# A mixture-of-experts kernel: small tiles moved as 128 rows, and the rotation tables made later on VectorE

## The chip, the cores and the metric

One core of one Trainium2 chip runs the whole program. The metric is the device time of one execution in microseconds (us), the median of the runs.

## The reference

Three blocks in a row on x of 4096 rows (tokens) by 256 columns: the same feed-forward layer twice, with a state-space layer between them.

```python
x = x + 0.5 * ffn(layernorm(x));  x = x + ssm(layernorm(x));  x = x + 0.5 * ffn(layernorm(x))
# ffn: each token goes to the one expert of E = 8 with the largest logit
router_probs = softmax(x @ Wr);  expert_idx = argmax(router_probs);  p_max = max(router_probs)
h = gelu(x @ W1[e] + b1[e]);  out = p_max * (h @ W2[e] + b2[e])      # D = 256, F = 1024
# ssm: N = 128 diagonal complex states, over the 4096 rows in order
h = a_disc * h + B_disc @ u_t;  y_t = Re(C @ h_t)
```

## The kernel before

The weights of all experts are loaded and split into two float16 parts at the start. A routing stage sorts the tokens by expert and makes a list of NT = 39 tiles of up to 128 tokens for each feed-forward layer. Tiles 0 to 31 have 128 slots. Tiles 32 to 38 have `width(q)` = 16 * (39 - q) slots: 112, 96, 80, 64, 48, 32 and 16. A slot with no token has the index 4095 for gathers and an index beyond the table for scatters, which the bounds check drops. A layer of the kernel is called the first (before the state-space layer) or the second.

Each layer's `ffn` is one loop over the tiles, written out on four engines that meet at semaphores:

- GpSimd (POOL) gathers the tile's rows of x (`xg`) and its records (`recf`) six tiles ahead, and scatters its result (`og`, two buffers). `fetch(q)` is two indirect DMAs at line 384, `scatter(q)` one at line 391. Its queue runs scatter(q), fetch(q + 6), scatter(q + 1), and so on.
- ScalarE (ACT) normalises (L521), writes the high half of the turned tile (L537), and applies the gelu, eight instructions per tile (L552).
- TensorE (PE) runs, in turn q: the transposes of tile q + 2 (L1135), `product1(q + 1)` (48 matmuls, L1160, as many columns as the tile is wide), and `product2(q)` (24 matmuls of 256 columns, L1180 to L1182). `product1(q + 1)` waits for VectorE's split of that tile; `product2(q)` for VectorE's split of the gelu output.
- VectorE (DVE) runs, in turn q: `split_x(q + 2)` (a register load of the expert's number, then L873), `split_h(q + 1)` (L885, L888, twice), `result(q)` (L902, L905, and in the first layer the statistics L908 and L909, after which it raises `o`, on which the scatter waits).

In the first layer VectorE also makes the tables `turn` and `back` of the state-space layer behind `result(q)`: `double(n)` (L705 to L708) doubles the table's length from n to 2n in four instructions; after nine of them it has 512 columns. Turns q = 8 to 16 hold double(1) to double(256); turn 18 clears `state` (L925); turns 20 and 22 hold the two `readout` calls (L714 and L715 over 512 columns each). Their first reader is VectorE itself in the state-space layer (L1016, L1028).

Behind the first layer SyncE (SP) waits for all scatters, then reads the rows back (L327). VectorE's next work, `negative_means` (L1008), waits for those loads.

Of the kernel before, what the change touches and what calls it, by code (L numbers as in the profile page):

```python
# [20 lines left out]
U32 = mybir.dt.uint32  # L21
# [7 lines left out]
T = 4096  # L29
D = 256  # L30
# [9 lines left out]
NT = NJ + E - 1  # L40
# [3 lines left out]
RW = D + 2  # L44
NB = E + 1
GR = 8
RING = 6
# [14 lines left out]
class Chain:  # L62
# [5 lines left out]
    def link(self, instruction):  # L68

        instruction.then_inc(self.sem, 1)  # L70
        self.n += 1
        self.engine.wait_ge(self.sem, self.n)


def macaron(nc, A):
# [3 lines left out]
    rec_dram = {ph: nc.dram_tensor(f"records_{ph}", [T, 4], F32, kind="Internal").ap() for ph in (1, 2)}  # L79
    x2_dram = nc.dram_tensor("x_after_ssm", [T, D], F32, kind="Internal").ap()  # L80
    ctx = ExitStack()
    with ctx:
        def sb(name, shape, dt=F32):
            return ctx.enter_context(nc.sbuf_tensor(name, shape, dt))
# [31 lines left out]
        state = sb("state", [P, 2])  # L116
# [16 lines left out]
        sorti = sb("sorti", [P, NT, 3], I32)  # L133
        eid = sb("eid", [P, NT], I32)

        def view(at, *shape, dt=F32):

            size = 1
            for s in shape:
                size *= s  # L140
            words = size // 2 if dt in (F16, BF16) else size
            assert at + words <= ARENA
            a = big[:, 2 * E * WB + 4 * at:2 * E * WB + 4 * (at + words)].bitcast(dt)
            names = "abcd"[:len(shape)]
            if len(shape) == 1:
                return a
            return a.rearrange("p (" + " ".join(names) + ") -> p " + " ".join(names),
                               **{n: s for n, s in zip(names, shape)})
# [26 lines left out]
        og = [view(6144 + k * RW, RW) for k in range(2)]  # L175
        xg = [view(8192 + k * D, D) for k in range(RING)]
# [15 lines left out]
        recf = sb("recf", [P, RING, 4])  # L192
# [60 lines left out]
        def width(q):  # L253

            return P if q < NJ else STEP * (NT - q)
# [83 lines left out]
        def _(pool):  # L339
# [27 lines left out]
            def ffn(ph, src, dst):  # L367
                s = S[ph]
                table = src
                pool.wait_ge(s["sorted_sb"], 1)  # L370
                if ph == 2:
                    for k in range(2):
                        pool.wait_ge(s_stored[k], 16 * (NC // 2))

                def fetch(q):

                    k, w = q % RING, width(q)
                    if q >= RING:
                        pool.wait_ge(s["o"], q - RING + 1)
                    for to, source, index in ((xg[k][0:w], table, 0), (recf[0:w, k, :], rec_dram[ph], 1)):  # L380
                        if index == 1 and q == 0:
                            pool.wait_ge(s["sorted_all"], 1)
                            pool.wait_ge(s["rec_stored"], 16)
                        pool.indirect_dma_start(to, None, source, bass.IndirectOffsetOnAxis(  # L384
                            ap=sorti[0:w, q, index:index + 1].bitcast(U32), axis=0)).then_inc(s["gath"][k], 16)

                def scatter(q):

                    w = width(q)
                    pool.wait_ge(s["o"], q + 1)  # L390
                    pool.indirect_dma_start(dst, bass.IndirectOffsetOnAxis(ap=sorti[0:w, q, 2:3].bitcast(U32), axis=0),  # L391
                                            og[q % 2][0:w, 0:RW if ph == 1 else D], None, bounds_check=T - 1, oob_is_err=False) \
                        .then_inc(s["scat"][q % RING], 16)

                for q in range(RING):
                    fetch(q)
                for q in range(NT):
                    scatter(q)
                    if q + RING < NT:
                        fetch(q + RING)  # L400
# [213 lines left out]
        def _(dve):  # L614
            chain = Chain(dve, dve_chain)
            link = chain.link
# [84 lines left out]
            def double(n):  # L701

                c0, s0 = turn[:, 0, 0:n], turn[:, 1, 0:n]
                cn, sn = turn[:, 0, n - 1:n], turn[:, 1, n - 1:n]
                dve.tensor_scalar(back[:, 0, 0:n], s0, sn, None, ALU.mult)  # L705
                link(dve.tensor_scalar(back[:, 1, 0:n], c0, sn, None, ALU.mult))
                dve.scalar_tensor_tensor(turn[:, 0, n:2 * n], c0, cn, back[:, 0, 0:n], ALU.mult, ALU.subtract)
                link(dve.scalar_tensor_tensor(turn[:, 1, n:2 * n], s0, cn, back[:, 1, 0:n], ALU.mult, ALU.add))  # L708

            def readout(part):  # L710

                col_a, col_b, how = (0, 1, ALU.subtract) if part == 0 else (1, 0, ALU.add)
                tmp = aa[:, part, :]
                link(dve.tensor_scalar(tmp, turn[:, col_b, :], col(15), None, ALU.mult))  # L714
                link(dve.scalar_tensor_tensor(back[:, part, :], turn[:, col_a, :], col(14), tmp, ALU.mult, how))  # L715
# [145 lines left out]
            def ffn(ph):  # L861
                s = S[ph]
                dve.wait_ge(owners, ph)
                experts = {}

                def split_x(q):

                    e = experts[q] = dve.value_load(eid[0:1, q:q + 1], min_val=0, max_val=E - 1)
                    w = width(q)
                    src = bank[6 + q % 2][:, 0:DC * P].rearrange("p (c t) -> p c t", c=DC)[:, :, 0:w]  # L870
                    sc = xscale[:, bass.ds(e, 1)]
                    dve.wait_ge(s["xt_hi"], q + 1)
                    dve.scalar_tensor_tensor(xts[q % 2][:, 1, :, 0:w], src, sc, xts[q % 2][:, 0, :, 0:w], ALU.mult, ALU.subtract) \  # L873
                        .then_inc(s["xt"], 1)

                def split_h(q):

                    sc = hscale[:, bass.ds(experts[q], 1)]
                    if q >= 2:
                        dve.wait_ge(s["m2"], q - 1)  # L880
                    for half in range(2):
                        f = slice(4 * half, 4 * half + 4)
                        dve.wait_ge(s["gelu"], q * 2 + half + 1)
                        of = slice(0, width(q))
                        dve.tensor_scalar(hs[q % 2][:, 0, f, of], hb[q % 2][:, f, of], sc, None, ALU.mult) \  # L885
                            .then_inc(s["h_hi"], 1)
                        dve.wait_ge(s["h_hi"], q * 2 + half + 1)
                        dve.scalar_tensor_tensor(hs[q % 2][:, 1, f, of], hb[q % 2][:, f, of], sc,  # L888
                                                 hs[q % 2][:, 0, f, of], ALU.mult, ALU.subtract).then_inc(s["hsplit"], 1)

                def result(q):

                    e = experts[q]
                    if q == 0:
                        dve.wait_ge(s["b2in"], 16)
                    dve.wait_ge(s["m2"], q + 1)
                    if q >= 2:
                        dve.wait_ge(s["scat"][(q - 2) % RING], (q - 2) // RING * 16 + 16)
                    w = width(q)
                    o, acc = og[q % 2][0:w, 0:D], bank[4 + q % 2][0:w, 0:D]  # L900
                    i2 = inv2[0:w, bass.ds(e, 1)]
                    dve.scalar_tensor_tensor(o, acc, i2, b2b[0:w, bass.ds(e * D, D)], ALU.mult, ALU.add) \  # L902
                        .then_inc(s["o_chain"], 1)
                    dve.wait_ge(s["o_chain"], q + 1)
                    last = dve.scalar_tensor_tensor(o, o, recf[0:w, q % RING, 2:3], xg[q % RING][0:w], ALU.mult, ALU.add)  # L905
                    if ph == 1:
                        link(last)
                        link(dve.bn_stats(stats[0:w, q % 2, :], o))  # L908
                        last = dve.bn_aggr(og[q % 2][0:w, D:D + 2], stats[0:w, q % 2, :])  # L909
                    last.then_inc(s["o"], 1)  # L910

                split_x(0)
                split_x(1)
                split_h(0)
                for q in range(NT):
                    if q + 2 < NT:
                        split_x(q + 2)
                    if q + 1 < NT:
                        split_h(q + 1)
                    result(q)  # L920
                    if ph == 1:
                        if 8 <= q < 17:
                            double(1 << (q - 8))
                        if q == 18:
                            link(dve.memset(state[:], 0.0))  # L925
                        if q in (20, 22):
                            readout((q - 20) // 2)

            entry_stats(3)
            weight_scales(0)  # L930
# [363 lines left out]
```

## Time and profile before

| | |
|---|---|
| median of 3 runs | 633.14 us (630.43 to 636.55) |
| profiled execution, own time | 628.32 us |
| its span | 626.4 us, mean granted TensorE clock 0.915 |
| TensorE, VectorE, ScalarE, GpSimd busy | 88%, 74%, 66%, 46% of the span |
| chain that ended last, by engine | TensorE 73%, VectorE 14% |

The span runs from the first to the last instruction; the execution's own time is 1.92 us more. A change of under 1% (6.3 us) can't be told from none by the measured times alone.

### The profile page before, as it was taken

Reading aid. Unit: us, or ns where it says so; the run is one execution under the profiler, and the core shown is the slowest. Engines: PE = TensorE matmul, PEld = TensorE weight load, DVE = VectorE, ACT = ScalarE, POOL = GpSimd, SP = SyncE. Lnnn points to the kernel's source line nnn. Section 1 sums busy time; section 2 is a strip of 40 time slices with the busy share of each in tenths; the row PEclk is TensorE's granted clock in tenths of the full one; section 3 lists DMA queues with packets and bytes.
Section 4 is the critical chain, followed back from the end, with each engine's and each line's share of the span. In section 5 each row is a group of like instructions: output and inputs, shape, how many; then the busy total and the mean of one; then the engine's idle time right before and its main releaser. Section 6 shows DMA issues by size and latency. Waiting matters only on the chain.

```text
span 626.4 us, 18541 instructions
## 1 busy us (share of the span) xinstructions
PE 548.9 (88%) x6476; PEld 500.8 (80%) x6476; DVE 465.1 (74%) x1001; ACT 412.1 (66%) x966; POOL 285.3 (46%) x326
## 2 busy tenths in 40 slices
PE   5990119999998999999989998799999999999991
PEld 5990019999998999999747776699999999999990
DVE  6759996888888888887529998576766666776760
ACT  3896997667675676677355663386667776667760
POOL 0042055555545455554245143555555555555521
PEclk9555558999999999999998989799999999999996
DMA  7999021111111111110081213111111111111100
GB/s 262 369 376 353 7 84 35 53 53 54 44 44 52 40 48 51 50 40 20 3 270 37 98 68 135 33 51 45 53 53 52 48 47 44 53 50 44 28 8 0
DMA packets 34616, 50.99 MB, mean 81 GB/s; under 512 B 6603, under 2 KB 27862, under 8 KB 34272
## 3 DMA queue, kind: packets, MB, share of 16 engines
q1 hardware_dynamic: 24800, 31.93, 14.9%
q0 software_dynamic: 9728, 17.89, 9.8%
q8 instruction: 55, 0.90, 0.6%
q14 instruction: 33, 0.27, 0.1%
HBM read 37.05 MB, written 13.67 MB: 81 GB/s over the span
## 4 chain that ended last, share of the span: by engine, by line
PE 73%; DVE 14%; issue 4%; DMA 3%; ACT 3%; SPq 1%; POOL 1%; POOLq 0%; DVEq 0%; ACTq 0%
PE banks L1160 31%; PE banks L1180 11%; PE banks L1182 11%; PE banks L1181 11%; PE banks L1093 3%; PE banks L1135 3%; DVE weights_arena L1019 3%; DMA weights_arena<-L_attn_u 2%; DVE weights_arena L662 2%; PE banks L1065 1%; DVE weights_arena L1016 1%; DVE weights_arena L1000 1%; ACT weights_arena L477 1%; DVE weights_arena L1028 1%; ACT weights_arena L468 1%
## 5 line engine op out<-in xcount | busy, mean ns | idle before, releaser
L552 ACT ACTIVATE weights_arena<-banks,b1t,inv 128x128 f32<-128x128 f32 (+7 forms) x624 | 220.7, 459 | 33.3 <-PE banks L1160 32.9
L1160 PE MATMUL banks<-weights_arena 128*128 128x128 f16 (+7 forms) x3744 | 206.9, 214 | 3.1 <-DVE weights_arena L873 2.0
L1160 PEld LDWEIGHTS banks<-weights_arena 128*128 x3744 | 199.3, 98 | 6.9 <-issue 5.9
L1180 PE MATMUL banks<-weights_arena 128*128 (+7 forms) x624 | 170.2, 273 | 0.0
L1182 PE MATMUL banks<-weights_arena 128*128 (+7 forms) x624 | 170.1, 273 | 0.0
L1181 PE MATMUL banks<-weights_arena 128*128 (+7 forms) x624 | 170.1, 273 | 0.0
L885 DVE TENSOR_SCALAR weights_arena<-weights_arena,hscale 128x512 f16<-128x512 f32 (+4 forms) x156 | 75.4, 483 | 54.5 <-ACT weights_arena L552 53.4
L888 DVE SCALAR_TENSOR_TENSOR weights_arena<-weights_arena,hscale 128x512 f16<-128x512 f32 (+4 forms) x156 | 109.9, 704 | 5.5
L537 ACT ACTIVATE weights_arena<-banks,xscale 128x256 f16<-128x256 f32 (+7 forms) x78 | 35.6, 456 | 92.3 <-PE banks L1135 89.9
L384 POOL DMA_INDIRECT recf<-records,sorti x78 | 83.3, 1067 | 23.8 <-issue 23.8
L391 POOL DMA_INDIRECT x_after_ffn<-weights_arena,sorti x39 | 39.4, 1010 | 82.9 <-DVE weights_arena L909 82.9
L391 POOL DMA_INDIRECT out<-weights_arena,sorti x39 | 39.1, 1003 | 75.3 <-DVE weights_arena L905 69.7
L1182 PEld LDWEIGHTS banks<-weights_arena 128*128 128x128 f16 (+7 forms) x624 | 62.4, 100 | 6.4
L1180 PEld LDWEIGHTS banks<-weights_arena 128*128 128x128 f16 (+7 forms) x624 | 62.4, 100 | 5.8
L1181 PEld LDWEIGHTS banks<-weights_arena 128*128 128x128 f16 (+7 forms) x624 | 62.4, 100 | 5.6
L873 DVE SCALAR_TENSOR_TENSOR weights_arena<-banks,xscale,weights_arena 128x256 f16<-128x256 f32 (+7 forms) x78 | 35.9, 460 | 41.3 <-issue 23.6
L384 POOL DMA_INDIRECT weights_arena<-L_attn_u,sorti x39 | 41.4, 1062 | 31.8 <-DVE sorti L854 20.2
L521 ACT ACTIVATE weights_arena<-weights_arena,recf 128x256 f32<-128x256 f32 (+7 forms) x78 | 46.1, 591 | 6.6 <-DMA recf<-records,sorti 6.6
L384 POOL DMA_INDIRECT weights_arena<-x_after_ssm,sorti x39 | 38.7, 992 | 17.0 <-issue 11.6
L902 DVE SCALAR_TENSOR_TENSOR weights_arena<-banks,inv,weights_arena 128x256 f32<-128x256 f32 (+7 forms) x78 | 37.3, 478 | 5.0 <-PE banks L1182 4.9
L662 DVE SCALAR_TENSOR_TENSOR weights_arena<-weights_arena,wscale 128x2048 f16<-128x2048 f32 x16 | 37.3, 2339 | 3.8 <-ACT weights_arena L477 3.7
L905 DVE SCALAR_TENSOR_TENSOR weights_arena<-weights_arena,recf 128x256 f32<-128x256 f32 (+7 forms) x78 | 37.8, 484 | 2.8
(216 smaller groups left out, 626.3 us busy)
## 6 DMA issues: line engine op xcount, KB each, us to landing
weights_arena<-L_ffn_W SPq DMA_DIRECT2D x16, 1024.0 KB, 12.7
weights_arena<-x_after_ffn SPq DMA_DIRECT2D x8, 516.0 KB, 7.4
weights_arena<-L_attn_u SPq DMA_DIRECT2D x8, 512.0 KB, 10.5
x_after_ssm<-weights_arena SPq DMA_DIRECT2D x8, 512.0 KB, 2.9
weights_arena<-L_ffn_b SPq DMA_DIRECT2D x2, 1024.0 KB, 5.2
recf<-records,sorti POOLq DMA_INDIRECT x78, 2.6
weights_arena<-L_attn_u,sorti POOLq DMA_INDIRECT x39, 3.0
x_after_ffn<-weights_arena,sorti POOLq DMA_INDIRECT x39, 2.5
```

Source lines behind the costliest of these rows:

```text
L384: pool.indirect_dma_start(to, None, source, bass.IndirectOffsetOnAxis(ap=sorti[0:w, q, index:index + 1].bitcast(U32), axis=0)).then_inc(s[ ...
L391: pool.indirect_dma_start(dst, bass.IndirectOffsetOnAxis(ap=sorti[0:w, q, 2:3].bitcast(U32), axis=0), og[q % 2][0:w, 0:RW if ph == 1 else ...
L521: act.activation(xng[q % 2][0:w], xg[q % RING][0:w], ACT.Identity, bias=recf[0:w, q % RING, 0:1], scale=recf[0:w, q % RING, 1:2]).then_inc ...
L552: last = act.activation(hb[q % 2][:, f, 0:width(q)], src, ACT.Gelu, bias=b1t[:, bass.ds(e * FC + f, 1)], scale=inv1[:, bass.ds(e, 1)])
L662: dve.scalar_tensor_tensor(lo, raw(e, which), wscale[:, n:n + 1], hi, ALU.mult, ALU.subtract) \
L885: dve.tensor_scalar(hs[q % 2][:, 0, f, of], hb[q % 2][:, f, of], sc, None, ALU.mult) \
L888: dve.scalar_tensor_tensor(hs[q % 2][:, 1, f, of], hb[q % 2][:, f, of], sc, hs[q % 2][:, 0, f, of], ALU.mult, ALU.subtract).then_inc(s["hs ...
L905: last = dve.scalar_tensor_tensor(o, o, recf[0:w, q % RING, 2:3], xg[q % RING][0:w], ALU.mult, ALU.add)
L1160: last = pe.matmul(acc[:, f * P:f * P + n_cols], weights[wpart * DC + d], xts[q % 2][:, xpart, d, 0:n_cols], start=(n == 0), stop=(n == 5))
L1180: pe.matmul(acc, hs[q % 2][:, 0, f, of], high, start=(f == 0), stop=False)
L1181: pe.matmul(acc, hs[q % 2][:, 0, f, of], low, start=False, stop=False)
L1182: last = pe.matmul(acc, hs[q % 2][:, 1, f, of], high, start=False, stop=(f == FC - 1))
```

## The change

Two edits. Every gather and scatter moves 128 rows, also for the seven narrow tiles, where it moved `width(q)`. The computation keeps its widths. And the doublings of the tables go from turns 8 to 16 to turns 28 to 36 (NT - 11 to NT - 3), the clearing of `state` and both readouts from turns 18, 20 and 22 to behind the last tile of the first layer; the clearing has no wait of its own any more.

```diff
 def fetch(q):
-    k, w = q % RING, width(q)
+    k = q % RING
...
-    for to, source, index in ((xg[k][0:w], table, 0), (recf[0:w, k, :], rec_dram[ph], 1)):
+    for to, source, index in ((xg[k], table, 0), (recf[:, k, :], rec_dram[ph], 1)):
...
-            ap=sorti[0:w, q, index:index + 1].bitcast(U32), axis=0)).then_inc(s["gath"][k], 16)
+            ap=sorti[:, q, index:index + 1].bitcast(U32), axis=0)).then_inc(s["gath"][k], 16)
 def scatter(q):
-    w = width(q)
...
-    pool.indirect_dma_start(dst, bass.IndirectOffsetOnAxis(ap=sorti[0:w, q, 2:3].bitcast(U32), axis=0),
-                            og[q % 2][0:w, 0:RW if ph == 1 else D], None, bounds_check=T - 1, oob_is_err=False) \
+    pool.indirect_dma_start(dst, bass.IndirectOffsetOnAxis(ap=sorti[:, q, 2:3].bitcast(U32), axis=0),
+                            og[q % 2] if ph == 1 else og[q % 2][:, 0:D], None, bounds_check=T - 1, oob_is_err=False) \
...
         if ph == 1:
-            if 8 <= q < 17:
-                double(1 << (q - 8))
-            if q == 18:
-                link(dve.memset(state[:], 0.0))
-            if q in (20, 22):
-                readout((q - 20) // 2)
+            if NT - 11 <= q < NT - 2:
+                double(1 << (q - NT + 11))
+    if ph == 1:
+        dve.memset(state[:], 0.0)
+        readout(0)
+        readout(1)
```

## Rows read from the trace of the kernel before

**Rows 1.** The page: busy time, share of the span, instructions.

```profile
PE 548.9 (88%) x6476; PEld 500.8 (80%) x6476; DVE 465.1 (74%) x1001; ACT 412.1 (66%) x966; POOL 285.3 (46%) x326
```

**Rows 2.** The chain that ended last, in order of time: start us, us, what.

```profile
100.21 2.69 PE banks L1160 x48
...
202.31 2.85 PE banks L1160 x48
...
285.01 1.83 PE banks L1160 x48
...
289.71 1.51 PE banks L1160 x48
...
294.08 1.30 PE banks L1160 x48
...
298.35 1.30 PE banks L1160 x48
...
302.38 1.29 PE banks L1160 x48
...
407.60 2.85 PE banks L1160 x48
...
606.19 1.31 PE banks L1160 x48
```

**Rows 3.** Timeline of VectorE: first instruction of a tile's turn; start us, us.

```profile
153.06 0.48 DVE L873 SCALAR_TENSOR_TENSOR weights_arena<-banks,xscale,weights_arena 128x256 f16<-128x256 f32 x1 [0.77 <-DVE turn L708]
...
158.92 0.48 DVE L873 SCALAR_TENSOR_TENSOR weights_arena<-banks,xscale,weights_arena 128x256 f16<-128x256 f32 x1 [0.79 <-DVE turn L708]
...
176.54 0.48 DVE L873 SCALAR_TENSOR_TENSOR weights_arena<-banks,xscale,weights_arena 128x256 f16<-128x256 f32 x1 [0.78 <-DVE turn L708]
...
182.50 0.48 DVE L873 SCALAR_TENSOR_TENSOR weights_arena<-banks,xscale,weights_arena 128x256 f16<-128x256 f32 x1 [0.78 <-DVE turn L708]
...
188.53 0.48 DVE L873 SCALAR_TENSOR_TENSOR weights_arena<-banks,xscale,weights_arena 128x256 f16<-128x256 f32 x1 [0.77 <-DVE turn L708]
...
194.76 0.48 DVE L873 SCALAR_TENSOR_TENSOR weights_arena<-banks,xscale,weights_arena 128x256 f16<-128x256 f32 x1 [0.78 <-DVE turn L708]
...
201.40 0.48 DVE L873 SCALAR_TENSOR_TENSOR weights_arena<-banks,xscale,weights_arena 128x256 f16<-128x256 f32 x1 [0.77 <-DVE turn L708]
...
212.36 0.48 DVE L873 SCALAR_TENSOR_TENSOR weights_arena<-banks,xscale,weights_arena 128x256 f16<-128x256 f32 x1 [0.78 <-DVE state L925]
...
217.37 0.48 DVE L873 SCALAR_TENSOR_TENSOR weights_arena<-banks,xscale,weights_arena 128x256 f16<-128x256 f32 x1 [0.56 <-issue]
...
261.08 0.48 DVE L873 SCALAR_TENSOR_TENSOR weights_arena<-banks,xscale,weights_arena 128x256 f16<-128x256 f32 x1 [0.56 <-issue]
```

**Rows 4.** Groups of VectorE by shape, 92 to 320 us: busy us, mean ns | idle.

```profile
L888 DVE SCALAR_TENSOR_TENSOR weights_arena<-weights_arena,hscale 128x512 f16<-128x512 f32 x64 | 48.1, 752 | 2.3
...
L885 DVE TENSOR_SCALAR weights_arena<-weights_arena,hscale 128x512 f16<-128x512 f32 x64 | 32.7, 512 | 5.0 <-ACT weights_arena L552 4.7
...
L888 DVE SCALAR_TENSOR_TENSOR weights_arena<-weights_arena,hscale 128x64 f16<-128x64 f32 x2 | 0.6, 284 | 0.1
...
L885 DVE TENSOR_SCALAR weights_arena<-weights_arena,hscale 128x64 f16<-128x64 f32 x2 | 0.5, 255 | 0.6 <-ACT weights_arena L552 0.6
```

**Rows 5.** Timeline of VectorE at the end of the first layer.

```profile
309.19 0.47 DVE L902 SCALAR_TENSOR_TENSOR weights_arena<-banks,inv,weights_arena 16x256 f32<-16x256 f32 x1 [0.98 <-PE banks L1182]
...
317.36 0.17 DVE L1008 TENSOR_SCALAR nb<-weights_arena 128x4 f32<-128x4 f32 x1 [6.54 <-DMA weights_arena<-x_after_ffn]
```

**Rows 6.** Timeline of GpSimd: the scatter beside the first readout.

```profile
222.63 1.23 POOL L391 DMA_INDIRECT x_after_ffn<-weights_arena,sorti  x1 [1.47 <-DVE weights_arena L909]
```

**Rows 7.** Line 391, first layer: ns min/median/max; landing us over both layers.

```profile
L391 POOL DMA_INDIRECT x_after_ffn<-weights_arena,sorti x39: 850/1012/1230, 109.2 to 311.6; - x39
...
DMA to landing us min/median/max: 1.8/2.5/4.0
```

**Rows 8.** DMA queues, 300 to 316 us: packets, MB, share.

```profile
q0 software_dynamic: 128, 0.00, 0.4%
```

## The prediction

> **What bounds the kernel now.** I read the page first, then the chain that ended last, then VectorE's timeline. TensorE is busy for 88% of the span [rows 1], and the chain runs through its matmuls nearly all the way through both feed-forward layers. The reader should look at the starts of `product1`: in the second layer they come every 5.52 us for full tiles, which is TensorE's own pace. From product1(1) to product1(38) the second layer takes 606.19 - 407.60 = 198.59 us, the first 302.38 - 100.21 = 202.17 us [rows 2]. The matmuls are the same, so the first layer loses 3.6 us somewhere.
>
> VectorE's timeline says where. Its turn without extra work is 217.37 - 212.36 = 5.01 us when it waits for nobody, 0.5 us under TensorE's 5.52. A turn with a doubling is longer than TensorE's: 158.92 - 153.06 = 5.86 us with double(2), (176.54 - 158.92) / 3 = 5.87 with each of double(4), (8) and (16), then 5.96, 6.03, 6.23 and 6.64 with double(32), (64), (128) and (256) [rows 3]. The extra over 5.01 is thus 0.86 us for the small ones, most of it fixed cost of four instructions and two waits, and 0.95, 1.02, 1.22, 1.63 for the last four. TensorE feels this once VectorE's lead is used up: product1(19) starts at 202.31, 0.91 us after the turn's first instruction at 201.40 [rows 2, 3], and it was waiting for just that instruction. So one number does the work below: product1(q + 2) can't start before the start of VectorE's turn q plus 0.91 us (0.48 is the instruction, 0.43 the way to TensorE).
>
> **What goes.** Turns 8 to 22 lose all extra work. Their turns fall to 5.01 us against 5.52, TensorE keeps its pace, and the first layer regains its 3.6 us. What is late next there is TensorE itself, so no more than this can be won.
>
> **What comes in turns 28 to 36.** The same nine doublings cost VectorE the same there, but the tiles get narrower from q = 32, and so does TensorE's turn. The starts of product1(34) to (38) are 285.01, 289.71, 294.08, 298.35, 302.38, so the turns are 4.70, 4.37, 4.27 and 4.03 us [rows 2]. VectorE's turn shrinks too. The split instructions fall from 752 to 284 ns and from 512 to 255 ns over seven steps of 16 tokens [rows 4], 0.067 and 0.037 each; twice a turn that is 0.20 us per step for `split_h(q + 1)`. `split_x(q + 2)` handles two columns per token where each split handles four, so half a step of 0.067, 0.03 us (an estimate from the same price per column). Its turns 30 to 35 without extra are then 4.98, 4.74, 4.51, 4.27, 4.04 and 3.81 us.
>
> Now add up from turn 28, which starts at 261.08 on the clock of before [rows 3] (TensorE's starts are kept on that clock too, the 3.6 us being taken off at the end):
> - turn 29 at 266.94 (+5.86), 30 at 272.81 (+5.87), 31 at 278.65 (+4.98 + 0.86), 32 at 284.25 (+4.74 + 0.86), 33 at 289.62 (+4.51 + 0.86), 34 at 294.84 (+4.27 + 0.95), 35 at 299.90 (+4.04 + 1.02), 36 at 304.93 (+3.81 + 1.22).
> - With the 0.91 us less 0.03 for each narrower step of its instruction, product1 may start, for tile 34, at 285.06 (before: 285.01), for 35 at 290.40 (+0.69), 36 at 295.58 (+1.50), 37 at 300.61 (+2.26), 38 at 305.61 (+3.23).
>
> VectorE's lead over TensorE thus covers double(1) to double(8) and is used up at turn 32 (285.06 against 285.01), before the long ones come, at the turns in which TensorE is fastest. Behind them, double(256) stands between `result(36)` and `split_h(38)`. Turn 36 without the next register load (0.56 us [rows 3]) is 3.57 - 0.56 = 3.0 us, with the doubling 4.63, so `split_h(38)` starts at 309.56, its first half is done at 310.1, and with 0.43 us for the way product2(38) starts at 310.5. Before, it started a turn behind product1(38), 302.38 + 4.03 = 306.4, and the last result's first instruction at 309.19 [rows 5], 2.8 us later. So the last result starts at 313.3 instead of 309.19: 4.1 us lost.
>
> **Both together:** -3.6 + 4.1 = +0.5 us. The cost moves, and is about as large at its new place, since the slack per turn is no larger (5.52 - 5.01 = 0.51 us for full tiles; 4.03 - 3.6 = 0.4 us for the narrowest).
>
> **The readouts behind the last tile.** Each is two instructions over 512 columns, by the same shapes some 0.75 + 0.51 us [rows 4], both 2.5 to 2.8 us with their waits. VectorE stands idle for 6.54 us there until the first rows are read back at 317.36 [rows 5]; they fit in. Without that cover they would cost the 2.8 us. The cleared `state` is small and has no wait of its own: nothing.
>
> But the last scatter is issued in this same stretch, and the way from it through the read-back is the path. Beside the first readout of before a scatter took 1.23 us [rows 6], against a median of 1.012 and a least of 0.850 (the last one, of 16 rows) [rows 7]. The Trainium skill, SBUF — State Buffer, section "SBUF: two separate sides", says that VectorE and GpSimd hold one port pair exclusively for a whole instruction, and that descriptors of GpSimd's DMAs can't be written meanwhile; the row with 1.23 us agrees in kind.
>
> **128 rows for narrow tiles.** GpSimd's instruction goes from 0.85 us (16 rows) towards 1.01 us (128 rows), 0.16 us at most per DMA [rows 7]. It is hidden for 20 of the 21 DMAs a layer (three for each of seven tiles): the gathers run six tiles ahead, the scatters have two turns until their buffer is wanted. GpSimd is busy for 46% [rows 1]. On the path it counts at the last scatter of each layer. The landing could at most go from 1.8 to the median of 2.5 us [rows 7]. The last four scatters moved 0.00 MB [rows 8]: with all their indices dropped, they have nothing to write, and the added slots are also dropped, so I take the landing unchanged (0) and keep 0.7 us per layer for the range. First layer: 1.23 - 0.85 = 0.38 us with the readout beside it; second: 0.16 us.
>
> **Sum** against the profiled execution of 628.32 us (span 626.4, the 1.92 us outside unchanged): -3.6 + 4.1 + 0.38 + 0.16 = +1.0, so 629.4 us. That execution was 0.8% faster than the median of the three runs; in the median's terms 633.1 + 1.0 = 634.1 us.
>
> **Rivals.**
> - *The early gain stays.* If doublings in the narrow turns cost less than in full ones, or VectorE's lead at turn 28 is larger, only a small part of the 4.1 us comes back: with 1 us lost, 634.1 - 3.1 = 631.0. For it: VectorE waited 0.98 us for TensorE before the last result [rows 5], so there is slack at the end. Against: that slack is counted above, and the fixed cost of a doubling has no reason to shrink. Chance 0.22.
> - *Slower, by the last scatter.* If the scatter's descriptors wait for both readouts, it starts its work when they end, some 2.6 us behind the last result, instead of 0.8 us: +1.8 us and the 0.16, for the 0.38 counted: 634.1 + 1.6 = 635.7. It decides if GpSimd can't slip in between two readouts' instructions. Against: 1.23 us beside such an instruction is only 0.2 us over the median. By the skill's rule named above (exclusive, for the whole instruction) the waiting would be of this kind. Chance 0.15.
> - *Slower, by the transfers.* 112 of 128 gathers of one tile ask for the same row 4095. If that or the dropped scatters land late, the last scatters pay up to 0.7 us each, and gathers nothing until they are six tiles (25 us) late: 635.5. Chance 0.08.
> - *The forecast* as summed, within a microsecond: 0.55.
>
> **How the numbers follow.** All four lie between 631 and 636 us, within 0.5% of each other and of no change. The runs themselves spread from 630.43 to 636.55. The range takes the cases' ends with about 2 us for the median of the runs: 629 to 638.5 us. Faster by over 1% would need more than the 6.3 us that the first layer doesn't have to give, so only scatter of the measurement gives it: 0.05. Slower by over 1% needs delays stacked on the forecast or scatter: 0.07. Within 1%: 0.88.
>
> **What the profile after would show.** Right: product1 starts every 5.52 us in turns 8 to 30 of the first layer with no wait for L873; waits of product1(35) to (38) and of product2(38) for VectorE; turns 28 to 36 at about 5.9 falling to 5.0 us; from product1(1) to product1(38) some 201.8 us; VectorE idle for some 4 us before L1008; the last scatter at 1.0 to 1.3 us. Wrong: no waits for VectorE in the last turns (first rival), or a last scatter of 2 us and more (second), or a landing over 2.5 us (third). A lower granted clock behind gaps in TensorE's work at 285 to 310 us would also spoil the sum.

## The result and the profile after

The changed kernel took 624.82 us (median of 20 runs, 623.07 to 631.65), the kernel before 631.95 us in the same series (20 runs, 628.70 to 639.32): a ratio of 0.989, 95% interval 0.9863 to 0.9916. The forecast was 634.1 us and its range began at 629.0. The change makes the kernel 7.1 us faster, and the prediction was wrong. Medians here are of all executions of a kernel, but a ratio with its interval leaves out those in a second, slower state, so it isn't always the quotient of the medians.

The profiled execution of after took 627.54 us, with a span of 625.8 us; that of before 628.32 and 626.4. These two differ by less than the medians, since two stretches outside the tile loops, from the start to product1(1) and between the layers, were 3.4 and 3.2 us longer in this execution of after. So the stages are compared, not the spans. The page of after, its first part, answers to [rows 1]:

```profile
span 625.8 us, 18542 instructions
...
PE 550.0 (88%) x6476; PEld 504.0 (81%) x6476; DVE 467.5 (75%) x1001; ACT 412.2 (66%) x966; POOL 288.9 (46%) x326
```

The chain that ended last, in after (start us, us, what), answers to [rows 2]:

```profile
103.63 2.68 PE banks L1159 x48
...
316.20 2.41 DMA x_after_ffn<-weights_arena,sorti
...
415.40 2.80 PE banks L1159 x48
...
613.95 1.29 PE banks L1159 x48
621.80 0.51 issue
622.31 1.21 POOLq L82
```

The end of the same chain in before. Its last piece starts at 614.77, and the reader should put that beside the span, which goes on to 626.4:

```profile
606.19 1.31 PE banks L1160 x48
...
613.02 0.48 DVE weights_arena L902
613.53 0.48 DVE weights_arena L905
614.07 0.70 issue
614.77 1.08 POOLq L82
```

From these rows and the timelines (first matmul of a product, first instruction of a scatter):

| stage, us | before | after |
|---|---|---|
| start to product1(1), first layer | 100.1 | 103.5 |
| first layer, product1(1) to product1(38) | 202.3 | 202.5 |
| product1(38) to the start of the last scatter | 9.3 | 10.2 |
| last scatter of the first layer | 0.85 | 1.27 |
| last scatter's start to product1(1) of the second layer | 96.0 | 99.2 |
| second layer, product1(1) to product1(38) | 198.5 | 198.5 |
| product1(38) of the second layer to the span's end | 20.3 | 11.9 |

The fourth row lies inside the fifth. The first and the fifth row are not the change. Where product1(1) starts goes with the clock of the execution, whatever the kernel: it was 99.8 to 101.1 us in the eleven traces with a mean granted clock of 0.92 or less, among them before and one of the change (change_third, 100.9), and 103.4 to 104.3 us in the nine with 0.966 or more, among them after and another of the change (change_again, 103.5). In the stretch from 18 to 62 us the granted clock (the third number from the end) was at half speed in before, its lower level of 1.2 GHz, and full in after; why the start takes longer at the full clock, no trace says:

```profile
18.00:62.00 44.00, 29.30 (x138) 28.28 (x138) 33.92 (x90) 37.17 (x37) 10.86 (x7) 0.51 1.06 371
```

```profile
18.00:62.00 44.00, 33.07 (x156) 32.04 (x154) 30.96 (x89) 36.82 (x36) 7.78 (x2) 1.00 1.06 370
```

The fifth row was 101.9 and 100.7 us in kernels with one of the two edits each (tables_only, rows_only, below), and 99.3 in extra_6, which up to there is the kernel before. What is left is +0.2, +0.9 and +0.4 us in the first layer, and -8.4 us behind the last product1 of all.

Of the 8.4 us, 8.2 are one instruction. GpSimd's queue ends with a DRAIN that the profile puts to line 82. In before it starts with the last scatter and runs for 11.4 us, to the end of the span; in after it takes 3.2 us. In the groups of line 82, of before (ns min/median/max, first and last start us):

```profile
L82 DVEq DRAIN  x1: 511/511/511, 613.5 to 613.5; - x1
L82 POOLq DRAIN  x1: 11443/11443/11443, 614.8 to 614.8; - x1
```

and of after:

```profile
L82 DVEq DRAIN  x1: 511/511/511, 621.3 to 621.3; - x1
L82 POOLq DRAIN  x1: 3210/3210/3210, 622.3 to 622.3; - x1
```

The scatters before it land as quickly as ever: 1.9 us at the median for the last five of before, so of its 11.4 us no more than 2 are landing. And the timeline of GpSimd in after shows something that before does not have, in both layers:

```profile
299.42 1.01 POOL L390 DMA_INDIRECT x_after_ffn<-weights_arena,sorti  x1 [3.95 <-DVE weights_arena L908]
306.55 1.00 POOL L390 DMA_INDIRECT x_after_ffn<-weights_arena,sorti  x1 [6.12 <-issue]
309.03 1.09 POOL L390 DMA_INDIRECT x_after_ffn<-weights_arena,sorti  x1 [1.48 <-DVE weights_arena L908]
...
607.90 1.00 POOL L390 DMA_INDIRECT out<-weights_arena,sorti  x1 [3.72 <-DVE weights_arena L904]
614.01 0.98 POOL L390 DMA_INDIRECT out<-weights_arena,sorti  x1 [5.11 <-issue]
615.92 0.98 POOL L390 DMA_INDIRECT out<-weights_arena,sorti  x1 [0.93 <-DVE weights_arena L904]
```

The rows with 6.12 and 5.11 us of idle time are the scatters of tile 35. Elsewhere in the second layer of after a scatter starts 0.8 to 0.95 us after the end of VectorE's last instruction for the result; here it starts 3.1 us after it, so 2.3 us late, for no reason that the profile names ("issue"). I call this the stop. GpSimd has time for it there, so it delays nothing. The experiments ask which edit shortens the DRAIN, and what the stop has to do with it.

### The profile page after: what moved, and what is told of

Same layout as the page of the kernel before. It is cut to its first block, busy times and chain, and to the rows that moved or that the text cites. A ratio compares the mean times of both kernels' runs of the same rounds, so it can differ in the third digit from the quotient of the medians.

```text
span 625.8 us, 18542 instructions
## 1 busy us (share of the span) xinstructions
PE 550.0 (88%) x6476; PEld 504.0 (81%) x6476; DVE 467.5 (75%) x1001; ACT 412.2 (66%) x966; POOL 288.9 (46%) x326
## 3 DMA queue, kind: packets, MB, share of 16 engines
q0 software_dynamic: 9984, 18.83, 11.2%
## 4 chain that ended last, share of the span: by engine, by line
PE 68%; DVE 19%; issue 5%; ACT 3%; DMA 2%; POOL 1%; DVEq 1%; SPq 0%; POOLq 0%; ACTq 0%
PE banks L1159 28%; PE banks L1179 10%; PE banks L1181 10%; PE banks L1180 10%; PE banks L1092 4%; DVE weights_arena L1018 3%; PE banks L1134 2%; PE banks L1064 2%; DVE weights_arena L661 2%; DVE weights_arena L1015 2%; DVE weights_arena L999 1%; ACT weights_arena L476 1%; DVE weights_arena L1027 1%; DVE weights_arena L884 1%; DVE weights_arena L904 1%
## 5 line engine op out<-in xcount | busy, mean ns | idle before, releaser
L884 DVE TENSOR_SCALAR weights_arena<-weights_arena,hscale 128x512 f16<-128x512 f32 (+4 forms) x156 | 77.4, 496 | 58.5 <-ACT weights_arena L551 57.3
L384 POOL DMA_INDIRECT recf<-records,sorti x78 | 84.6, 1084 | 23.8 <-issue 23.8
## 6 DMA issues: line engine op xcount, KB each, us to landing
weights_arena<-L_attn_u SPq DMA_DIRECT2D x8, 512.0 KB, 10.2
```

## The experiments

Kernels were run in five groups. Each group has its own runs of the kernel before. In the second to fourth group that kernel took 661 to 678 us, with longer turns of TensorE. Nothing measured here says why; it isn't the chip's number alone, which was the same in the second group (678.27 us) and the fifth (632.79 us). So times are compared within a group, and the DRAIN, the stop and the time from the last product1 to the end (on which all agree) between groups.

### First group: which edit (before 633.15 us)

`rows_only` has the 128 rows, and the tables where they were; `tables_only` has the tables' move alone. `scatters_128` and `gathers_128` are before with half of the rows edit each.

```diff
 rows_only: the diff of the change without its last part;  tables_only: its last part alone
 scatters_128:
-            ap=sorti[0:w, q, 2:3].bitcast(U32), axis=0), og[q % 2][0:w, 0:RW if ph == 1 else D], ...
+            ap=sorti[:, q, 2:3].bitcast(U32), axis=0), og[q % 2] if ph == 1 else og[q % 2][:, 0:D], ...
 gathers_128:
-    for to, source, index in ((xg[k][0:w], table, 0), (recf[0:w, k, :], rec_dram[ph], 1)):
+    for to, source, index in ((xg[k], table, 0), (recf[:, k, :], rec_dram[ph], 1)):
-            ap=sorti[0:w, q, index:index + 1] ...
+            ap=sorti[:, q, index:index + 1] ...
```

> The kernel before with 128 rows in every gather and scatter, tables where they were. Theory T (the gain is GpSimd's closing drain, 11.4 us in the trace of before and 3.2 us in that of the change, and it comes from the 128-row DMAs): the drain is about 3 us again and the time is 8 us under before, ratio about 0.987. Rival R (the drain's length belongs to the execution, not to the program, and the gain is made in the first layer by the tables): the drain varies and the ratio is 1.000 to 1.001.

> The kernel before with the rotation tables at turns 28 to 36 and behind the last tile, narrow DMAs as before. Theory T: drain 11.4 us as before; the first layer from product1(1) to its last scatter about 1 us longer than before's 211.6; time 0.5 to 1 us over before, ratio 1.001. Rival R: ratio 0.989.

> The kernel before with 128 rows in the scatters alone. If the drain clears up what dropped or missing slots of the scatters left, it falls to 3 us here and the time by 8 us. If the gathers alone do it, it stays at 11.4 us. If each narrow DMA adds its share, it falls by a third, to about 8.7 us.

> The kernel before with 128 rows in the gathers alone. If each narrow DMA adds its share to the drain, 28 of 42 are gone and it falls by two thirds, to about 6 us; if scatters alone matter, it stays at 11.4 us; if any narrow DMA at all makes the drain long, 11.4 us too.

| | median us | ratio (95%) | DRAIN us | last product1 to end us | product1(38) to last scatter, first layer |
|---|---|---|---|---|---|
| rows_only | 623.59 | 0.985 (0.979 to 0.990) | 3.2 | 11.9 | 9.3 |
| tables_only | 634.19 | 1.001 (0.998 to 1.004) | 11.4 | 20.3 | 10.2 |
| scatters_128 | 634.42 | 1.002 (0.998 to 1.006) | 11.0 | 19.8 | 9.3 |
| gathers_128 | 628.90 | 0.993 (0.989 to 0.996) | 3.0 | 14.0 | 11.7 |

The gain is the rows edit's, and nearly all of it is in the DRAIN. Line 82 of rows_only and of tables_only, one under the other:

```profile
L82 POOLq DRAIN  x1: 3214/3214/3214, 620.1 to 620.1; - x1
```

```profile
L82 POOLq DRAIN  x1: 11438/11438/11438, 622.2 to 622.2; - x1
```

Within the rows edit, the gathers do it: 128 rows in the scatters alone leave 11.0 us. That speaks against the first idea, that the DRAIN pays for the small scatters just in front of it. The gathers shorten it although the last one was issued six tiles (some 25 us) before. But they bring the stop to another place, the last scatter of each layer. GpSimd's timeline in gathers_128, the last scatters of both layers:

```profile
308.66 0.87 POOL L391 DMA_INDIRECT x_after_ffn<-weights_arena,sorti  x1 [3.11 <-DVE weights_arena L909]
313.63 0.87 POOL L391 DMA_INDIRECT x_after_ffn<-weights_arena,sorti  x1 [4.10 <-issue]
...
615.23 0.87 POOL L391 DMA_INDIRECT out<-weights_arena,sorti  x1 [3.13 <-DVE weights_arena L905]
620.08 0.85 POOL L391 DMA_INDIRECT out<-weights_arena,sorti  x1 [3.98 <-issue]
```

There it costs 2.4 us in the first layer (11.7 instead of 9.3) and 2.2 us in the second (14.0 instead of 11.9). So the stop is a real wait of GpSimd. tables_only shows neither stop nor gain, and the 0.9 us of the third row of the stage table.

### Second group: where the rows count, and how many (before 678.27 us)

All are the changed kernel with narrower gathers, as below (written short here and in the next groups), except `spaced`, which is the changed kernel with its nine doublings spread over turns 2, 5, ..., 26.

```diff
 narrow_layer1, narrow_layer2 (w = width(q) in that layer, 128 in the other):
+    rows = w if ph == 1 else P          # narrow_layer2: ph == 2
-    ... ((xg[k], table, 0), (recf[:, k, :], rec_dram[ph], 1)):
+    ... ((xg[k][0:rows], table, 0), (recf[0:rows, k, :], rec_dram[ph], 1)):
 all_112:
+    rows = P if q < NJ else P - STEP    # 112 rows for tiles 32 to 38, both layers
 spaced:
-            if NT - 11 <= q < NT - 2:
-                double(1 << (q - NT + 11))
+            if q % 3 == 2 and q < 27:
+                double(1 << (q // 3))
```

> The changed kernel with width(q) rows in the first layer's gathers alone. If the drain only knows of what was issued shortly before, it stays at 3.2 us. If shares add up over the program, 7 us.

> The changed kernel with width(q) rows in the second layer's gathers alone. If the drain only knows of what was issued shortly before it (no narrow gather of the first layer), it is 11 us as before. If each narrow gather adds its share, half the difference: 7 us.

> The changed kernel with 112 rows in all 14 gathers of each layer's narrow tiles: as many gathers under 128 rows as before, but 448 rows missing in place of 1792. If the drain grows with the number of such gathers it is 11 us; if with the missing rows, 3.2 + 8.2 / 4 = 5.3 us; if it wants less than some width, 3.2 us.

> The changed kernel with the nine doublings at turns 2, 5, 8, ..., 26 instead of 28 to 36, readouts still behind the last tile. By the sum of the prediction (0.51 us of slack in a full turn, a lead of 2 us, doublings of 0.86 to 1.63 us) three turns pay for each one: product1(1) to product1(38) takes 198.5 us as in the second layer, the stretch from product1(1) to the last scatter 4.1 to 4.4 us less than the changed kernel's 212.7, time about 620.6 us, ratio to before about 0.982. If the doublings cost TensorE nothing where they are now, nothing changes against the changed kernel (0.989).

narrow_layer2 ran in 671.61 us (0.9997, 0.9947 to 1.0046): the whole gain was gone, with no stop in the second layer and this DRAIN:

```profile
L82 POOLq DRAIN  x1: 11010/11010/11010, 658.7 to 658.7; - x1
```

narrow_layer1 ran in 663.07 us (0.989, 0.980 to 0.997), with 3.2 us:

```profile
L82 POOLq DRAIN  x1: 3230/3230/3230, 658.9 to 658.9; - x1
```

So only the second layer's gathers matter for the DRAIN, and what is counted in the first layer is not carried over: the stop of narrow_layer1's second layer stands at tile 35, as in the change. all_112 (665.18 us; 0.990, 0.985 to 0.994) had a DRAIN of 3.9 us and its stop at tile 37: 224 rows less put the stop two tiles later. So it isn't a matter of each gather being full or not, for which 112 rows would be as narrow as 16. spaced ran in 664.20 us (0.987, 0.982 to 0.991), with 9.3 us from product1(38) to the last scatter of the first layer, as before the change. The 198.5 us that were expected from product1(1) to product1(38) did not show: it took 220.1 us, in a group in which this stretch of the second layer too was 208.1 us long.

### Third and fourth group: a count of rows, or of DMAs (before 660.69 and 676.42 us)

Again the changed kernel with narrower gathers in the second layer: that of the last tile alone (`narrow_last_one`, both its gathers), of the last four tiles (`narrow_last_four`), the records alone (`narrow_records2`) or x alone (`narrow_x2`). The four narrow ones were run once each. With them the change and spaced were timed again in both groups (change_again, change_third, spaced_again, spaced_third).

```diff
 narrow_last_one:  rows = w if ph == 2 and q == NT - 1 else P       # both gathers
 narrow_last_four: rows = w if ph == 2 and q >= NT - 4 else P       # both gathers
 narrow_records2:  (xg[k], table, 0), (recf[0:w, k, :] ...) in layer 2
 narrow_x2:        (xg[k][0:w], table, 0), (recf[:, k, :] ...) in layer 2
```

> The changed kernel with 16 rows in the two gathers of the second layer's last tile alone. If one gather far under 128 rows at the end is enough for the long drain, 11 us. If the drain grows with the missing rows of the second layer (224 of 896 here), 3.2 + 7.8 / 4 = 5.2 us. If it grows with the number of narrow gathers, 4.3 us.

> The changed kernel with width(q) rows in the second layer's record gathers (16 bytes a row) alone, the gathers of x at 128. If both kinds of gather count alike for the drain, half of the 7.8 us: 7.1 us. If the gathers of x (1 KB a row) make it, 3.2 us; if any narrow one is enough, 11 us.

> The changed kernel itself as the partner of the run above: ratio 0.989 to before, closing drain 3.2 us, first layer 212.7 us from product1(1) to its last scatter.

> The doublings at turns 2 to 26 once more, beside the changed kernel itself in the same job, since the last job's chip ran the kernel before 7% slower too. As before: product1(1) to product1(38) of the first layer 198.5 us, the stretch to the last scatter 4.1 to 4.4 us shorter than the changed kernel's. If the doublings cost nothing where the change puts them, both kernels are alike.

> The changed kernel with width(q) rows in the second layer's gathers of x alone (448 rows missing). Theory M (what the end costs grows with the rows missing in the second layer, of whatever kind: 0 rows 0 us, 224 rows 1.0 us, 448 rows 2.2 to 2.3 us, 896 rows 7.9 us, 1344 rows 8.4 us over the changed kernel's 11.9 us from product1(38) to the end less the last turn): 2.3 us more than the changed kernel, before or in the drain. Rival X (the gathers of x make the long drain): drain 11 us, 7.9 us more.

> The changed kernel with width(q) rows in both gathers of tiles 35 to 38 of the second layer (704 rows missing, 8 narrow gathers). Theory M: between the 2.3 us of 448 rows and the 7.9 us of 896, 5 us if it is smooth; a step to one of the two if a threshold lies between. Rival W (the widths 112 to 80 of tiles 32 to 34 make it): nothing or 1 us.

> The changed kernel itself as the partner of the run above: drain 3.2 us, ratio about 0.987 to before.

> The doublings at turns 2 to 26 against the changed kernel in one job. On a chip where TensorE's turns are the 5.52 us of the trace of before, product1(1) to product1(38) takes 198.5 us (changed kernel 202.5), the rest up to the last scatter 9.3 us (10.2), so 4 to 5 us or 0.7% less than the changed kernel. Where TensorE stalls on its own (the last two jobs, turns over 5.52 us), VectorE's lateness is partly hidden and the gain is 1 to 2 us.

narrow_last_one (654.25 us) had a DRAIN of 4.0 us and the stop at tile 37; narrow_records2 (655.16) and narrow_x2 (663.75) 3.2 us each and the stop at the last tile, though the one narrows 16-byte records and the other rows of x: bytes don't count, rows do. narrow_last_four (672.61) had no stop, and

```profile
L82 POOLq DRAIN  x1: 10918/10918/10918, 659.7 to 659.7; - x1
```

The last scatters of narrow_x2, with the stop before the last one:

```profile
653.88 0.98 POOL L391 DMA_INDIRECT out<-weights_arena,sorti  x1 [3.02 <-DVE weights_arena L905]
658.73 0.98 POOL L391 DMA_INDIRECT out<-weights_arena,sorti  x1 [3.87 <-issue]
```

The change took 652.57 and 660.02 us in these groups (0.985, 0.980 to 0.990; 0.984, 0.976 to 0.991), spaced 649.28 and 661.51 (0.984, 0.979 to 0.989; 0.982, 0.974 to 0.991). product1(38) to the last scatter was 10.4 and 10.3 us in the change, 9.3 in spaced both times. But product1(1) to (38) was 214.6 us in the change against 213.6 in spaced in one group and 217.7 against 219.3 in the other: this varies more than what the doublings can cost. The 1.0 us of the late doublings between product1(38) and the last scatter is shown, that spaced is faster as a whole is not. The 4 to 5 us that were expected of it go with turns of 5.52 us, which no run of spaced had.

### Fifth group: more gathers in the kernel before (before 632.79 us)

By then one count fitted all runs: in each layer, the rows of all GpSimd's DMAs plus 16 for each DMA. GpSimd stops at the scatter with which the sum reaches 16384. The kernel before has 13632 rows and 117 DMAs in a layer, a sum of 15504. A gather of 128 records more adds 144: six give 16368, seven 16512. `extra_6` and `extra_7` are the kernel before with that many gathers into a tensor that nobody reads, in turns 10 to 15 or 16 of the second layer; SyncE waits for them at the end too.

```diff
+    if ph == 2 and 10 <= q < 10 + EXTRA:
+        pool.indirect_dma_start(spill[:, q - 10, :], None, rec_dram[2], bass.IndirectOffsetOnAxis(
+            ap=sorti[:, q, 1:2].bitcast(U32), axis=0)).then_inc(extra_in, 16)
```

> The kernel before with six more gathers of 128 records in the second layer, behind tiles 10 to 15, into a spare buffer that nothing reads. Theory C (GpSimd makes one stop of 3.1 us in a layer once its count, rows of all its DMAs in that layer plus 16 for each DMA, reaches 16384; where a layer ends without it, the closing drain takes 11 us in place of 3.2): 15504 + 6 x 144 = 16368 is 16 short, so no stop and a drain of 11.4 us, time as before. Rival N (some number of 128-row DMAs or of missing rows near the end decides): the same here.

> The same with seven. Theory C: 16512, the count passes 16384 at the scatter of tile 36 (16432 with it, 16368 before it); a stop of 3.1 us ahead of that scatter, the closing drain 3.2 us, and 7 to 8 us less time than with six (about 0.988), though one DMA more is issued and every narrow tile still moves width(q) rows. Rival N (the missing rows of the narrow tiles make the drain long): drain 11.4 us, no difference from six.

extra_6 took 633.04 us (1.001, 0.997 to 1.005), extra_7 627.38 us (0.992, 0.988 to 0.997). One gather more of 2 KB makes the kernel 5.7 us faster. Line 83 (the same DRAIN, one line on) in extra_6, then in extra_7:

```profile
L83 POOLq DRAIN  x1: 11193/11193/11193, 619.0 to 619.0; - x1
```

```profile
L83 POOLq DRAIN  x1: 5563/5563/5563, 620.5 to 620.5; - x1
```

and GpSimd's scatter of tile 36, in extra_6 and then in extra_7, at which the sum passes 16384 in the latter (16432 with it, 16368 before it):

```profile
616.62 0.87 POOL L395 DMA_INDIRECT out<-weights_arena,sorti  x1 [3.13 <-DVE weights_arena L912]
```

```profile
615.83 0.89 POOL L395 DMA_INDIRECT out<-weights_arena,sorti  x1 [4.91 <-issue]
```

The place of the stop and the sign of the gain came out as the count says. The sizes did not: the DRAIN took 5.6 us where 3.2 was expected, the whole gain was 5.7 us instead of 7 to 8, and the scatter at the stop started 2.6 us after its result, not 3.1 as at every other stop of a second layer.

### All second layers together

| sum of the second layer | kernels | stop at the scatter of tile | DRAIN us | last product1 to end us |
|---|---|---|---|---|
| 15504 | before, tables_only | none | 11.4 | 20.3 |
| 15952 | scatters_128, narrow_layer2 | none | 11.0 | 19.8 |
| 16144 | narrow_last_four | none | 10.9 | 19.7 |
| 16368 | extra_6 | none | 11.2 | 20.0 |
| 16400 | gathers_128, narrow_records2, narrow_x2 | 38 | 3.0 to 3.2 | 14.0 to 14.2 |
| 16512 | extra_7 | 36 | 5.6 | 14.3 |
| 16624 | all_112, narrow_last_one | 37 | 3.9 to 4.0 | 12.9 |
| 16848 | change, rows_only, narrow_layer1, spaced | 35 | 3.2 | 11.9 to 12.0 |

Each tile in the third column is where the running sum first reaches 16384. For the change: 78 gathers and 36 scatters of 128 rows are 114 DMAs, 114 * 144 = 16416, and the 36th scatter is that of tile 35. The 16 per DMA is fitted. From where the stops stood in gathers_128 (not at tile 37, 14512 rows and 116 DMAs) and extra_7 (at tile 36, 14480 rows and 122 DMAs) it must be over 5.3, and from extra_6's having none (14400 rows and 123 DMAs, against 14528 and 117 in gathers_128) under 21.3. Rows alone are excluded by these.

The short DRAINs differ less than the column says. Where the stop was at tile 35, 37 or 38, the DRAIN ended 2.8 to 3.0 us after the last scatter's start, and 0.9 us after its landing (1.9 us for 16 rows, 2.1 for 128). It is 3.9 to 4.0 us long where the stop was at tile 37, since there it begins 0.9 us before the last scatter and not 0.2. Without a stop it ended 10.7 to 11.2 us after that start. Only extra_7, with 5.3 us, lies between.

## Why the prediction was wrong

**The step that failed** is in the part "128 rows for narrow tiles": "On the path it counts at the last scatter of each layer", which gave +0.16 us in the second layer, and for the end the sum's "span 626.4, the 1.92 us outside unchanged". It took what lies behind the last scatter for its landing (1.8 to 2.5 us) and costed the edit by the DMAs' own durations. The trace of before had the number that contradicts this: the last scatter starts at 615.0 and the span ends at 626.4, 11.4 us later, of which landing is 1.9. The prediction didn't ask what the other 9 are. No rival held them either, and so the range stopped at 629.0. In place of +0.16 the runs showed -8.4 us, 8.2 of it in GpSimd's closing DRAIN (rows_only against before and tables_only; narrow_layer2 against narrow_layer1). The sentence that "faster by over 1% would need more than the 6.3 us that the first layer doesn't have to give" looked in one place only.

**The early turns** held. Turns 8 to 22 of after run at TensorE's own pace, two starts of product1 5.51 us apart where a doubling's turn took 5.86 and more before [rows 3]. Timeline of TensorE in after:

```profile
180.73 2.84 PE L1159 MATMUL banks<-weights_arena 128*128 128x128 f16 x48
...
186.24 2.84 PE L1159 MATMUL banks<-weights_arena 128*128 128x128 f16 x48
```

**The doublings in turns 28 to 36** held, turn by turn. VectorE's timeline of after, which answers to [rows 3, 5]; the first instruction of turns 29, 30 and 36, and that of the last result:

```profile
267.04 0.48 DVE L872 SCALAR_TENSOR_TENSOR weights_arena<-banks,xscale,weights_arena 128x256 f16<-128x256 f32 x1 [0.77 <-DVE turn L707]
...
272.89 0.45 DVE L872 SCALAR_TENSOR_TENSOR weights_arena<-banks,xscale,weights_arena 128x224 f16<-128x224 f32 x1 [0.78 <-DVE turn L707]
...
305.21 0.25 DVE L872 SCALAR_TENSOR_TENSOR weights_arena<-banks,xscale,weights_arena 128x32 f16<-128x32 f32 x1 [0.78 <-DVE turn L707]
...
313.79 0.47 DVE L901 SCALAR_TENSOR_TENSOR weights_arena<-banks,inv,weights_arena 16x256 f32<-16x256 f32 x1 [1.28 <-PE banks L1181]
```

Measured against the second layer, which has no such work, before had lost 3.7 us by product1(26); after has lost nothing up to product1(33) and then 4.0 us up to product1(38), where the prediction gave back 3.6 and took 3.2. Turn 29 takes 5.85 us (5.87 forecast), and from turn 29 to 36 it is 38.2 us (38.0 forecast). TensorE waits for VectorE from product1(34) on, as forecast, and for `split_h(38)` behind double(256). Its timeline, product1(34) to (38) and the first matmul of product2(38):

```profile
285.21 1.89 PE L1159 MATMUL banks<-weights_arena 128*128 128x80 f16 x48 [0.52 <-DVE weights_arena L872]
...
290.73 1.57 PE L1159 MATMUL banks<-weights_arena 128*128 128x64 f16 x48 [0.75 <-DVE weights_arena L872]
...
295.89 1.37 PE L1159 MATMUL banks<-weights_arena 128*128 128x48 f16 x48 [0.73 <-DVE weights_arena L872]
...
300.91 1.36 PE L1159 MATMUL banks<-weights_arena 128*128 128x32 f16 x48 [0.69 <-DVE weights_arena L872]
...
305.97 0.68 PE L1159 MATMUL banks<-weights_arena 128*128 128x16 f16 x21 [0.97 <-DVE weights_arena L872]
...
310.84 0.27 PE L1179 MATMUL banks<-weights_arena 128*16 x1 [0.78 <-DVE weights_arena L887]
```

So "-3.6 + 4.1 = +0.5" measures +0.2 to product1(38) (forecast 3.23 - 3.6 = -0.4) and +0.9 from there to the last scatter (forecast 4.1 - 3.23 = +0.9), together +1.1. Of the 0.6 us that the first is off, 0.3 are there when turn 29 starts: VectorE's lead was a little smaller than counted. spaced and rows_only, which have no doubling there, show the 9.3 us of before, and so tie the 0.9 to the late doublings; that it is double(256) among them rests on its place in front of `split_h(38)` and on the wait in the last row above. The first rival fell by these waits. The granted clock did not fall behind these gaps: 1.00 from 264 to 316 us.

**The readouts** fit into VectorE's idle time (they end at 317.9 us; the last scatter lands at 318.6, and only then are rows read back), and the last scatter beside them took 1.27 us where 1.23 was forecast [rows 6, 7]; without them, in rows_only, 0.98. The second rival wanted the scatter to wait until both readouts, 2.6 us, had ended. It was 0.3 us longer, no more. The Trainium skill, SBUF — State Buffer, section "SBUF: two separate sides", has the loser of that port pair fully blocked for a whole instruction of the other, where VectorE's has two inputs in SBUF or runs in a two-port mode. The first readout's 0.75 us instruction had 0.4 us to go when the scatter started at 316.20, so 0.3 us neither contradicts that nor proves it.

**The transfers** (third rival) were not late: 2.41 us from the last scatter's start to its landing, 1.27 us of them the instruction itself, against 1.84 in the chain of before. The last scatter's landing thus grew by 0.6 us, 0.4 of them counted.

**The balance** in the medians: +1.5 us in the first layer (0.2, 0.9 and 0.4) and -8.4 at the end give -6.9; measured -7.1 (by the interval of the ratio, a gain of 5.3 to 8.7 us). Cause and place of the gain are shown. What GpSimd does in the stop, why a layer without a stop has a closing DRAIN some 8 us longer, why the count starts anew with a layer (between them GpSimd waits for SyncE's loads and for VectorE's tables), and why extra_7's took 5.6 us, stays open; the profile names nothing there but "issue" and DRAIN. What it is that GpSimd counts is open too: rows plus a fixed amount per DMA fits all the stops, and no more is shown.

The rows edit alone, with the tables left where they were, came to 0.985 (0.979 to 0.990) of before, against 0.989 (0.986 to 0.992) for the whole change in its own series. The intervals overlap, so that the tables' move costs anything is shown by the stages (+0.2 and +0.9 us) and not by the times.

## What to carry to other kernels

Read the span to its very end: subtract the start of the last DMA and its landing from the span, and if microseconds are left, look at which engine's closing DRAIN holds them and what it depends on. An edit that adds rows to many indirect DMAs is to be costed by their sum over a layer too, not only by one instruction's duration. And when work is moved from where an engine has half a microsecond of slack per turn, look for that slack at the new place, turn by turn; here that gave the time from product1(1) to product1(38) to 0.6 us.

## What was not expected of the hardware

- GpSimd's closing DRAIN took 11.4 us behind 117 indirect DMAs of 13632 rows in the last layer, and 3.2 us behind 117 DMAs of 14976 rows. More rows made it shorter.
- Once rows plus 16 per DMA reach 16384 in a layer (seen at 16400, not at 16368), one scatter of GpSimd starts 3.1 us after its result instead of 0.8 to 1.0 (2.6 us in extra_7); at the last scatter this costs 2.2 to 2.4 us.
- A scatter whose indices are all dropped takes 0.98 us for 128 rows and 0.85 us for 16, and has landed 2.1 us and 1.9 us after its start: the last three of after moved 0.00 MB, and still it costs almost what a full one does.
- One gather of 2 KB more (extra_7 against extra_6) made the kernel 5.7 us faster.
